# One attention kernel on one core: score transposes as 64-row tiles of the array, with engine orders moved

## What is computed

```python
Q = einsum('bse,hec->bhsc', X, Wq) + bq   # 16 heads, 2 x 64 columns
K = einsum('bse,hec->bhsc', X, Wk) + bk
V = einsum('bse,hed->bhsd', X, Wv) + bv
A1 = Q1 @ K1.T * s ; A2 = Q2 @ K2.T * s   # the two halves of Q and K
P = softmax(A1) - lam * softmax(A2)
O = P @ V
Y = concat_heads(O) @ Wo + bo
```

## Time and profile before

| | us |
|---|---|
| three runs | 1275.02, 1275.51, 1275.62 (median 1275.51) |
| the profiled execution's own time | 1274.62 |
| its span, first to last instruction | 1272.8 |
| PE busy / POOL / ACT / DVE | 1213.6 / 1017.1 / 963.2 / 903.8 |
| mean granted TensorE clock | 0.994 of full speed |

### The profile page before, as it was taken

How to read it: one execution, slowest core, us unless ns; L and a number is a source line. 1 busy time by engine, 2 the same in 40 slices (tenths; PEclk the granted TensorE clock), 3 DMA queues, 4 the chain that set the end, 5 groups by cost and what they waited for, 6 DMA issues and landing times.

```text
span 1272.8 us, 23640 instructions
## 1 busy us (share of the span) xinstructions
PE 1213.6 (95%) x7682; PEld 767.5 (60%) x7682; DVE 903.8 (71%) x1537; ACT 963.2 (76%) x1709; POOL 1017.1 (80%) x654
## 2 busy tenths in 40 slices
PE   3887999999999999999999999999999999998998
PEld 2654556666656666555666555666555666664688
DVE  7975677777777777777777777777777777775420
ACT  2285788888888888888888888888888888886432
POOL 3199998988888888888988888888889888889200
PEclk9998999999999999999999999999999999998999
DMA  6841111111111111221111121112111111110000
GB/s 142 317 109 42 47 43 28 29 46 47 46 46 41 46 46 46 47 46 28 24 46 46 46 47 41 46 46 46 46 46 33 24 41 46 42 42 1 1 18 18
DMA packets 74115, 63.36 MB, mean 50 GB/s; under 512 B 45156, under 2 KB 63076, under 8 KB 74084
## 3 DMA queue, kind: packets, MB, share of 16 engines
q1 hardware_dynamic: 73076, 62.78, 19.9%
q10 hardware_dynamic: 880, 0.19, 0.1%
q0 software_dynamic: 128, 0.01, 0.0%
HBM read 19.96 MB, written 9.44 MB: 23 GB/s over the span
## 4 chain that ended last, share of the span: by engine, by line
PE 83%; POOL 8%; DVE 4%; ACT 3%; issue 2%; DMA 0%; ACTq 0%; DVEq 0%; POOLq 0%
PE ps L481 29%; PE ps L494 20%; PE ps L508 17%; PE ps L435 6%; PE ps L520 4%; POOL p_mix L392 4%; PE ps L569 3%; PE ps L556 2%; POOL work L389 2%; ACT p_mix L664 1%; PE ps L463 1%; ACT work L664 1%; POOL w L376 1%; DVE pt L797 1%; DVE small L841 0%
## 5 line engine op out<-in xcount | busy, mean ns | idle before, releaser
L841 DVE TENSOR_REDUCE small<-ps 128x1 f32<-128x1024 f32 x512 | 624.1, 1220 | 243.3 <-PE ps L481 243.2
L392 POOL TENSOR_TENSOR p_mix<-p_mix,work 128x1024 f32<-128x1024 f32 x256 | 610.0, 2383 | 21.3
L677 ACT ACTIVATE pt<-ps 128x512 f32<-128x512 f32 x512 | 306.8, 599 | 206.5 <-PE ps L494 204.9
L389 POOL TENSOR_SCALAR work<-work,small 128x1024 f32<-128x1024 f32 x256 | 306.7, 1198 | 114.3 <-DVE small L871 114.3
L494 PEld LDWEIGHTS ps<-ident,p_mix 128*128 128x128 f32 x2048 | 220.3, 141 | 226.0 <-issue 172.2
L494 PE MATMUL ps<-ident,p_mix 128*128 128x128 f32 x2048 | 331.1, 284 | 20.2 <-POOL p_mix L392 15.2
L664 ACT ACTIVATE p_mix<-ps,small 128x1024 f32<-128x1024 f32 x256 | 284.4, 1111 | 17.9 <-DVE small L841 17.9
L664 ACT ACTIVATE work<-ps,small 128x1024 f32<-128x1024 f32 x256 | 286.0, 1117 | 0.6 <-DVE small L841 0.6
L508 PE MATMUL ps<-pt,v_h 128*64 128x512 f32 x1024 | 249.3, 608 | 0.0
L481 PE MATMUL ps<-k_hi,q_hi 64*128 64x512 f32 x512 | 233.0, 455 | 8.4 <-ACT p_mix L664 2.3
L481 PE MATMUL ps<-k_hi,qx_hi 64*128 64x512 f32 x512 | 233.6, 456 | 0.0
(11 more groups left out here) (133 smaller groups left out, 1242.0 us busy)
## 6 DMA issues: line engine op xcount, KB each, us to landing
qx_hi<-q_hi SPq DMA_DIRECT2D x64, 256.0 KB, 3.7
qx_lo<-q_lo SPq DMA_DIRECT2D x64, 256.0 KB, 4.7
v_scratch<-pt SPq DMA_DIRECT2D x16, 512.0 KB, 3.5
v_h<-v_scratch SPq DMA_DIRECT2D x32, 256.0 KB, 3.2
wqk_raw<-in_L_attn_Wk SPq DMA_DIRECT2D x31, 64.0 KB, 1.7
wqk_raw<-in_L_attn_Wq SPq DMA_DIRECT2D x31, 64.0 KB, 1.9
x_all<-in_L_attn_X SPq DMA_DIRECT2D x2, 512.0 KB, 4.8
wo_dup<-in_L_attn_Wo SPq DMA_DIRECT2D x2, 512.0 KB, 8.8
```

Source lines behind the costliest of these rows:

```text
L389: pool.tensor_scalar(e2, e2, l_inv[:, 2 * km + 1:2 * km + 2], l1_neg[:, km % 4:km % 4 + 1], ALU.mult, ALU.mult).then_inc(scaled, 1)
L392: pool.tensor_tensor(e1, e1, e2, ALU.add).then_inc(mix_done, 1)
L677: act.activation(pt4[:, kb % 2, half * 4:half * 4 + 4, j * P:(j + 1) * P], pt_ps.rearrange("p (c q) -> p c q", c=4), ACT.Copy).then_inc(pt ...
L841: dve.tensor_reduce(neg_max[:, m:m + 1], slot[SLOT[k, s]], AX.X, ALU.max, negate=True)\
```

## The change

In the turn, a transpose reads 64 queries x 128 keys, in the upper 64 rows of the array for the first turn and in the lower 64 for the second. A turn has eight of them, one for each chunk of 128 keys, and fills the same PSUM bank as before with 8 x 64 columns. An empty instruction that can't be merged into another stands ahead of each turn. ScalarE copies the bank to the 64 query columns of all eight chunks.

The orders: on TensorE, at j = 2, the first turn goes between the two score tiles. On ScalarE the high part is written at the start of the next step instead of the end of its own. On VectorE the reciprocals come ahead of both row maxima at j = 3, between them at j = 2, and after them at j = 0 and 1; the low part comes ahead of the second row maximum; the P·V copy is written at the end of the step j = 0 instead of the start of j = 1; the addition to y moves from j = 2 to the end of j = 1.

```diff
@@ tensor: turn @@
                 after(pe, pt_evac, 2 * n + half)
-                for c in range(4):
-                    col = (k - LAG) % 4 * S + (half * 4 + c) * P
-                    mm = pe.transpose(pt_ps[:, c * P:(c + 1) * P], p_mix[:, col:col + P], ident[:, :])
+                pe.nop(nofuse=True)
+
+                rows = slice(half * D, (half + 1) * D)
+                for c in range(KC):
+                    col = (k - LAG) % 4 * S + c * P
+                    mm = pe.transpose(pt_ps[:, c * D:(c + 1) * D], p_mix[rows, col:col + P], ident[rows, rows])
                 mm.then_inc(pt_ready, 1)
@@ tensor: step @@
                     scores(g, k, 0)
-                    scores(g, k, 1)
+                    if j != 2:
+                        scores(g, k, 1)
                 if now(g, k, LAG):
                     turn(g, k, 0)
+                if j == 2 and now(g, k):
+                    scores(g, k, 1)
@@ scalar: evac_pt @@
-                act.activation(pt4[:, kb % 2, half * 4:half * 4 + 4, j * P:(j + 1) * P],
-                               pt_ps.rearrange("p (c q) -> p c q", c=4), ACT.Copy).then_inc(pt_evac, 1)
+                act.activation(pt4[:, kb % 2, :, j * P + half * D:j * P + (half + 1) * D],
+                               pt_ps.rearrange("p (c q) -> p c q", c=KC), ACT.Copy).then_inc(pt_evac, 1)
@@ scalar: step @@
+                p = k - 1
+                if p % TB in PROJ_AT and now(g, p, -TB):
+                    high_part(g * 2 + p // TB + 1, (p // TB + 1) % 2, PROJ_AT.index(p % TB),
+                              slot[SLOT[p, "proj"]])
                 if now(g, k, LAG):
                     evac_pt(g, k, 0)
...
-                if k % TB in PROJ_AT and now(g, k, -TB):
-                    high_part(n, par, PROJ_AT.index(k % TB), slot[SLOT[k, "proj"]])
@@ vector: step @@
-                if j == 1 and now(g, k - j, 2 * QB):
-                    dve.wait_ge(pv_done, g * (BODY // QB) + kb - 1)
-                    dve.tensor_copy(o_t[:, (kb % 2) * BANK:(kb % 2 + 1) * BANK], o_ps).then_inc(o_evac, 1)
-                if now(g, k):
-                    row_max(g, k, 0)
-                if now(g, k, 1):
+                def inv_sums():
                     dve.wait_ge(exp_done, 2 * m + 2)
                     after(dve, scaled, m - 3)
                     dve.reciprocal(l_inv[:, r:r + 2], l_sum[:, l:l + 2]).then_inc(recip_done, 1)
                     dve.tensor_scalar(l1_neg[:, e:e + 1], l_sum[:, l:l + 1], lam_neg, None, ALU.mult)\
                         .then_inc(recip_done, 1)
+
+                if j == 3 and now(g, k, 1):
+                    inv_sums()
                 if now(g, k):
-                    row_max(g, k, 1)
-                if j == 2 and now(g, k - j, 2 * QB):
-                    add_y(g, kb)
+                    row_max(g, k, 0)
+                if j == 2 and now(g, k, 1):
+                    inv_sums()
                 p = k - 1
                 if p % TB in PROJ_AT and now(g, p, -TB):
                     low_part(g * 2 + p // TB + 1, (p // TB + 1) % 2, PROJ_AT.index(p % TB),
                              slot[SLOT[p, "proj"]])
+                if now(g, k):
+                    row_max(g, k, 1)
+                if j < 2 and now(g, k, 1):
+                    inv_sums()
+                if j == 0 and now(g, k - j, 2 * QB):
+                    dve.wait_ge(pv_done, g * (BODY // QB) + kb - 1)
+                    dve.tensor_copy(o_t[:, (kb % 2) * BANK:(kb % 2 + 1) * BANK], o_ps).then_inc(o_evac, 1)
+                if j == 1 and now(g, k - j, 2 * QB):
+                    add_y(g, kb)
```

## The result

The changed kernel takes 1227.2 us (1226.4 to 1227.5, 4 runs) against 1275.6 for the kernel before in the same session: ratio 0.962, 95% interval 0.9603 to 0.9636. That is 48.4 us less; 1244 was forecast, 31.5 less. Direction and range held; the gain is half as large again as the sum gave.

A forecast was written before the change was run, and what follows sets the result against it. PE was taken as the bound, busy 95%, with even heads of 34.64 us. The terms summed to -1.1 a head, -32 over 29 heads, so 1242.7 from the profiled 1274.62, forecast as 1244; range 1219 to 1287.

The forecast's parts named there:

- (a): Transposes in 64-row shape: fewer changes of array shape between turns and neighbouring blocks on PE, -1.40 us a head.
- (b): Eight transposes a turn instead of four, at 0.0585 us each: +0.48 us a head.
- (c): Edge from turn to scores: first score load outlasts the last transpose by 0.05 us, +0.50 a head.
- (d): First turn ahead of the second score tile in step 2 stalls 0.16 us for ACT's evacuation, +0.33 a head.
- (e): PE's waits for an exp in step 3 and a DVE subtraction at step 0 or 4 go: -1.0 us a head.
- (g): Empty instruction, 16 a head: taken as 0, at most 0.05 us each, 0.8 a head if all are exposed.
- rival A: Inside every turn, transpose loads aren't hidden: spacing 0.11 us instead of 0.0585, +5.5 a head, about 1435; chance 0.16.
- Rival D: Drain between scores and transposes belongs to transpose mode, not array shape: +0.6 us a head, 1293; chance 0.02.
- Rival C: More gain: (c) and (d) cost nothing, -1.9 us a head, 1220; chance 0.10.
- Rival B: Half the gain: stalls stay or are replaced, 1263, or empty instructions are exposed, 1267; chance 0.14.
- Unchanged: 0: The ends, POOL-bound heads and the feed-forward part, were to keep their time: 0 us.
- (f): Moves of ACT's high part, y additions, reciprocals and output copy: no cost on PE, though reciprocals come 1.2 us later.

The follow-up runs named there:

- e3: The changed kernel with three empty instructions ahead of each turn instead of one: 1227.6 us.
- e7: The changed kernel with turns and scores interleaved by row half on TensorE, both score tiles before the first turn in every step: 1219.3 us.
- e4: The changed kernel with the halves swapped, first turn in the lower 64 rows and second in the upper: 1236.9 us.
- e1: The changed kernel with TensorE's and VectorE's orders of the kernel before, 64-row turns kept: 1262.5 us.
- e6: The changed kernel with VectorE's order of the kernel before: 1278.3 us.
- e2: The kernel before, with its 128-row transposes, given the new orders of TensorE and VectorE: 1278.2 us.
- e8: The kernel before, with its 128-row transposes, given VectorE's new order alone: 1269.1 us.
- e9: The changed kernel with TensorE's and VectorE's orders of before, except the low part moved ahead of the second row maximum: 1218.2 us.
- e5: The changed kernel with TensorE's order of before at j = 2, both score tiles and then the first turn: 1220.8 us.

## Why the prediction was right in kind and short by a third

By its own steps, per head:

| step | forecast | measured |
|---|---|---|
| (a) changes of shape | -1.40 | -1.40: 0.14, 0.15 and 0.20 at V and O as priced |
| (b) eight transposes | +0.48, spacing 0.0585 | +1.0, spacing 0.0625, a turn 0.50 |
| (c) turn to scores | +0.50 | about -1.0 |
| (d) turn in step 2 | +0.33 | +0.74 |
| (e) stalls | -1.0 | -1.1 to -1.2: what the other rows leave of the sum, not measured by itself |
| (g) empty instruction | 0 | not shown; two more don't change the time (e3) |
| sum | -1.1 | -1.81 |

- **The step that failed is (c).** I priced the edge from a turn to the scores between 0 and 0.05 lost, with "the half of the array that the turn doesn't use could load early" as the best case. The other half does more than load: it streams. The scores stream 0.36 after the turn's first transpose (632.65 to 633.01), although the turn takes 0.50, and the lead is kept, since the next turn needs only the half that is free first. That is 0.14 gained at each of ten edges a head, where 0.05 was to be lost, less 0.2 twice at the projection, which needs both halves. It turns +0.50 into -1.0, and this 1.5 is more than the whole surplus of 0.7. e7 bears it out (both halves at work for 1.96 us), and e4, where the lead is smaller by one transpose.
- **(b) and (d) were too low,** by 0.9 together, and so hid part of the miss in (c); that 1244 lies no further off is in part luck. The spacing is 0.0625, 0.004 over my figure. The break-even spacing of rival A, 0.067, was computed with (c) as a loss; with (c) as a gain it lies at about 0.077. And because the upper half is free earlier, the turn in step 2 waits longer for the same copy: from the first stream of the turn ahead, at 636.12, to 637.54 it is 1.42, forecast 1.38, while the upper half is free after 1.05, forecast 1.22.
- **Rival A fell.** Eight transposes in one row group go at 0.0625, not 0.11: loads overlap streams of the same rows, in the 64-row shape too. The rule of the Trainium skill that gives it (TensorE: Matmul & The Clock Gate, "Packing small matmuls": loads overlap only across row groups) doesn't hold for these instructions; by it a turn would take about 0.9 (an estimate, eight times the 0.11 of load and stream), and the trace has 0.50.
- **Rival D fell.** The drain went with the shape: the first turn's record starts at 634.40, as the upper half's last score matmul ends (634.17 and 0.23).
- **Rival C has the nearest number, 1220, but not for its reason:** it takes (c) and (d) as free, and (c) was a gain and (d) a loss.
- **Rival B didn't come true here.** It describes e1 and e6, where stalls take most or all of the gain because an order isn't fitted.
- **"Unchanged: 0" for the ends was wrong by 3 us,** most of it in GpSimd's head 1. It goes with VectorE's order and not with the turns: 46.3 and 46.5 in e1 and e6, which have the order of before, 49.5 and 48.1 in e2 and e8, which have 128-row turns and the new one. The cause stays open. The later reciprocals of (f) are an obvious suspect, but e9, which has them in their old place, still needs 48.2, and e3, with the orders of the changed kernel, 48.0.

## What to carry to other kernels

Price row tiles of the array as two engines, not one: work in the upper and the lower 64 rows runs at once, even if it belongs to different stages, and a few instructions out of program order; let the stage that follows begin in the half that is left free, and deal both halves' work out in the program. Look at the completion of the first tile too, which such an order can delay (e7). A shape change saved is worth its drain only if no wait stands behind it: the same turns were worth 1.0% with the old orders and 3.8% with VectorE's new one (e8 to e5), and of that order one moved instruction is enough (e9). Test the moves of a combined change one by one: e9, with that move alone, is 9 us faster than the changed kernel with all of them.

## What was unexpected of the hardware

- A matmul in the free row half started, with its weight load, ahead of three transposes that the program has before it (632.90 against 632.96), and in e4 the second score matmul ahead of the first (602.91 against 603.06).
- Transposes of 64 columns keep their spacing (0.0625) while the other half streams scores, and score matmuls keep theirs (0.23).
- With 16 short transposes a step instead of 8 longer ones the granted clock stays at 1.00 in the even heads. In GpSimd's head 1, where PE is busy 38.36 of 49.47, its mean was 0.86 (before: 0.93 with 36.37 of 46.29).
